# Decoder kernel, one core: order of key powers, residual bases, first table and first values in attention 1, and where the gate's exponential is computed

## The chip, the cores and the metric

The kernel runs on one core of one Trainium2 chip. The metric is the time of one execution in device microseconds. TensorE (PE) multiplies and transposes into PSUM, VectorE (DVE), ScalarE (ACT) and GpSimd (POOL) work element by element, SyncE (SP) issues most transfers. Every engine takes its own instructions in order and waits at semaphores.

## The reference

Six sub-layers, each followed by a layer norm over the last axis, on x of 8 batches x 128 tokens x 128 features, all float32. The change touches the first three.

```python
x = _layernorm(x + _L0_attn_ref(x, ...))       # returns x + attention(LN(x)) @ w_out + b_out
x = _layernorm(x + _L0_xattn_ref(x, ctx, ...)) # q, k layer-normed per head of 8; context of 77 rows
x = _layernorm(x + _L0_ffn_ref(x, ...))        # 8 experts, 2 chosen per batch from the mean token
x = _layernorm(x + _L1_attn_ref(x, ...))       # router: attention for 32 tokens, a scan for 96
x = _layernorm(x + _L1_xattn_ref(x, ctx, ctx, mask, ...))
x = _layernorm(x + _L1_ffn_ref(x, ...))
```

Both attentions have 16 heads of 8 features and a softmax. In the first, the input of the layer norm is 2x + b_out + product. In the second, each key's 8 features are scaled with 1/sqrt(variance + eps) of their head: 77 rows x 8 batches x 16 heads, that is 128 columns of 77 rows. The third takes `gate = softmax(mean(x) @ gate_w.T)`, the two largest of eight, normalised.

## The kernel before, in words

All work of the first attention (`at1`) is a loop over 8 batches, written out by hand on each engine (`attention_tensor`, `attention_vector`, `attention_scalar`, `attention_pool`). In step i, TensorE computes `shifted(i)` (scores less their maxima, L1443 and L1446), `weigh(i-1)` (exponentials by values, L1462), `flips(i)` (projection of batch i-3, L1473, and transposes of the maxima of batch i+1, L1477, and of the normalised output of batch i-2, L1480), `scores(i+2)` (L1422), and transposes outputs (L1508). VectorE in step i makes, in this order: R of batch i-3 (L974, residual base XB plus projection), the maxima of batch i+2 (L952) with the reciprocal and normalisation of batch i-1 (L983, L995) between them, the first remainder (L962), X of batch i-4 (L1004, needs `rstd` from GpSimd), the second remainder (L962), then the statistics of R down to the variance `ve` (L1010 to L1012). `between` holds further work for the end of a step: `key_variances` (L932, L935), `weights2`, `weights5`. ScalarE takes the exponentials (L641), outT (L652) and the flipped maxima (L657).

GpSimd runs one queue: constants and zeroed values, `spread8` (L520), `residual1` (whole XB = 2x + b, L540, L541), `key_squares` (L526, after the last context copy), three key powers of 32 columns (L534, each waits for `k_ss`), then `attention_pool(at1, ...)`: the power for `rstd` of each batch (L504) and behind those of batches 0 and 1 a key power of 16 columns. After it come the query squares (L557), `residual2` (whole XB = X + bp2, L546), `attention_pool(at2)` and the column mask (L562 and the selection behind it).

In the opening, TensorE transposes x and the context, makes q1, k1 and both halves of v1 (L1391), then the scores of batch 0; three context products (`kv.0` to `kv.2`, L1391 again), the scores of batch 1, the first flip; then step 0, in which the last context product stands. ScalarE copies x0T and ctxT (L614), k1 with the head mask (L620), kv.0 to kv.2 (L683, L684), and only then the first flip (L657). VectorE copies q1 (L1036) and v1 (L1039). A ring (`Ring`) hands PSUM banks to fill/copy pairs in the order of `ACT_JOBS` and `DVE_JOBS`; a fill waits until the last copy from its bank is done.

In the gated mixture VectorE ranks the 8 logits (L1094 to L1107) while ScalarE loads the exponential's table, computes `e8`, and loads the Gelu table again (L726 and the loads around it); VectorE makes `c8` (L1115); TensorE spreads it (L1627, L1630). Meanwhile TensorE has done `residual(0)` (L1620) and two of four hidden products of the second half (L1385), the other two come after `residual(1)`.

## Time and profile before

| | us |
|---|---|
| median of 3 runs | 433.56 (433.10 to 434.45) |
| the profiled execution, its own time | 434.33 |
| its span in the profile | 432.5 |

| engine | busy us | share |
|---|---|---|
| PE | 391.3 | 90% |
| DVE | 280.9 | 65% |
| ACT | 235.6 | 54% |
| POOL | 130.5 | 30% |

The profile is of one execution. 1.83 us of its time lie outside the span. A timeline line gives the start from the start of the span, the length of the group, the engine, the line of the kernel, the instruction, what it writes from what, and in brackets how long the engine sat idle before it and what ended that. A group of several instructions (x4) is one line; the engine need not be busy between them. The share of busy time of TensorE holds filler matmuls too (L1371), which the kernel issues to keep the engine's clock up.

### The profile page before, as it was taken

To read this page: it belongs to the slowest core of one execution; us is meant where nothing else is said; L and a number is where in the kernel's file an instruction comes from. 1 tells how busy PE (TensorE), PEld (TensorE's weight loads), DVE (VectorE), ACT (ScalarE), POOL (GpSimd) and SP (SyncE) were. 2 spreads that over 40 slices of the span, in tenths; PEclk is the share of its full clock that TensorE was granted. 3 is DMA by queue.
4 is the path that set the end of the run, shared out by engine and by line. 5 is a ranking of instruction groups with operands and counts; after the bars stand their busy time and mean duration, and the time that the engine had idled before them with its cause. 6 is when DMAs were issued, how large, how long until landed. Compare 5 with 4: busy or idle time off the path is not lost.

```text
span 432.5 us, 10063 instructions
## 1 busy us (share of the span) xinstructions
PE 391.3 (90%) x4041; PEld 262.1 (61%) x4050; DVE 280.9 (65%) x705; ACT 235.6 (54%) x441; POOL 130.5 (30%) x120
## 2 busy tenths in 40 slices
PE   5989798889999999977999999898999899999992
PEld 2556566546675946555676767645777466666662
DVE  6769656754765586897799897732566544444446
ACT  1855444736668267799999993025555442222220
POOL 6936952300113050004889893100011100000001
PEclk9999979999999999999999999989999999999998
DMA  6320000000000000020223220450000000000001
GB/s 176 74 49 2 4 2 2 1 2 3 3 5 0 2 0 2 6 109 23 90 89 102 93 81 2 131 163 2 3 4 4 2 0 0 2 0 1 2 0 48
DMA packets 16881, 13.84 MB, mean 32 GB/s; under 512 B 6548, under 2 KB 14133, under 8 KB 16837
## 3 DMA queue, kind: packets, MB, share of 16 engines
q1 hardware_dynamic: 15538, 12.51, 10.0%
q10 hardware_dynamic: 1299, 0.71, 0.5%
q8 instruction: 32, 0.52, 0.5%
q14 instruction: 12, 0.10, 0.1%
HBM read 12.64 MB, written 0.57 MB: 31 GB/s over the span
## 4 chain that ended last, share of the span: by engine, by line
PE 69%; ACT 11%; DVE 10%; POOL 5%; issue 4%; POOLq 0%; DVEq 0%; ACTq 0%
PE PS L1830 9%; PE PS L1909 6%; PE PS L1913 6%; PE PS L1940 6%; PE PS L1385 5%; PE PS L1443 5%; PE PS L1817 4%; POOL hr L534 4%; ACT att L641 3%; PE PS L1422 3%; PE PS L1371 2%; PE PS L1391 2%; PE PS L1508 2%; PE PS L1462 2%; ACT outT L652 2%
## 5 line engine op out<-in xcount | busy, mean ns | idle before, releaser
L641 ACT ACTIVATE att<-PS 77x512 f32<-77x512 f32 (+1 forms) x96 | 51.7, 591 | 47.2 <-PE PS L1446 47.2
L952 DVE TENSOR_REDUCE mxp<-PS 128x4 f32<-128x308 f32 (+1 forms) x96 | 48.0, 536 | 34.3 <-PE PS L1422 34.3
L878 ACT ACTIVATE kM<-PS 128x512 f32<-128x512 f32 x32 | 19.1, 597 | 55.5 <-PE PS L1909 54.4
L504 POOL TENSOR_TENSOR rstd<-ve,neg_half 128x1 f32<-128x1 f32 x24 | 13.1, 547 | 114.6 <-DVE ve L1012 114.6
L1258 DVE TENSOR_TENSOR_SCAN big<-big,PS 128x768 f32<-128x768 f32 x22 | 38.1, 1743 | 3.4 <-PE PS L1817 3.3
L1324 DVE TENSOR_TENSOR big<-kM,PS 128x512 f32<-128x512 f32 x32 | 21.9, 687 | 27.3 <-PE PS L1913 26.0
L498 POOL TENSOR_TENSOR rstd<-ve,neg_half 128x4 f32<-128x4 f32 x6 | 6.2, 1029 | 102.2 <-DVE ve L908 102.2
L1909 PE MATMUL PS<-xT,V 128*128 128x512 f32 x64 | 33.0, 597 | 1.1 <-DVE xT L1312 0.8
L1913 PE MATMUL PS<-xT,V 128*128 128x512 f32 x64 | 32.7, 592 | 0.0
L1940 PEld LDWEIGHTS PS<-big 128*128 128x128 f32 x256 | 29.7, 192 | 3.3 <-issue 3.3
L1371 PE MATMUL PS<-negsel,identb 128*128 128x512 bf16 x101 | 26.1, 400 | 6.1 <-DVE negsel L1024 4.4
L1940 PE MATMUL PS<-big 128*128 128x128 f32 x256 | 29.7, 275 | 0.0
L1446 PE MATMUL PS<-flipped,negsel 32*77 32x128 bf16 (+1 forms) x384 | 24.8, 219 | 0.0
L831 ACT ACTIVATE att<-big,BT 128x256 f32<-128x256 f32 x58 | 24.6, 497 | 0.0
L534 POOL TENSOR_TENSOR hr<-hvar,half_bh 77x32 f32<-77x32 f32 (+1 forms) x5 | 22.0, 4419 | 7.0 <-DVE hvar L935 7.0
L1345 DVE SCALAR_TENSOR_TENSOR R<-PS,aff,R 128x128 f32<-128x128 f32 x56 | 15.8, 345 | 11.2 <-PE PS L1940 11.2
L1443 PE MATMUL PS<-qT,kM 32*77 32x128 f32 x512 | 20.8, 276 | 1.8 <-ACT att L641 1.1
L1371 PEld LDWEIGHTS PS<-negsel,identb 128*128 128x128 bf16 x109 | 10.4, 102 | 19.1 <-issue 4.9
L1913 PEld LDWEIGHTS PS<-xT,V 128*128 128x128 f32 x64 | 12.2, 190 | 15.3 <-issue 14.8
L657 ACT ACTIVATE flipped<-PS 128x128 f32<-128x128 f32 (+1 forms) x33 | 10.7, 325 | 18.2 <-PE PS L1477 10.0
L1817 PE MATMUL PS<-ident,att 128*128 128x128 f32 x128 | 19.3, 273 | 1.2 <-ACT att L831 1.2
L1258 DVE TENSOR_TENSOR_SCAN untransposed<-untransposed,PS 128x768 f32<-128x768 f32 x10 | 17.5, 1748 | 4.4 <-PE PS L1817 4.1
(368 smaller groups left out, 894.6 us busy)
## 6 DMA issues: line engine op xcount, KB each, us to landing
kM<-Cdram SPq DMA_DIRECT2D x6, 384.0 KB, 3.5
XH<-Cdram SPq DMA_DIRECT2D x5, 384.0 KB, 3.3
xT<-Cdram SPq DMA_DIRECT2D x5, 384.0 KB, 3.4
V<-in_L_ffn_Wg SPq DMA_DIRECT2D x1, 1024.0 KB, 5.4
V<-in_L_ffn_Wu SPq DMA_DIRECT2D x1, 1024.0 KB, 8.0
out_x<-X SPq DMA_DIRECT2D x2, 256.0 KB, 2.3
ctxN<-in_ctx ACTq DMA_DIRECT2D x1, 308.0 KB
X<-in_x ACTq DMA_DIRECT2D x1, 256.0 KB, 4.0
```

The source lines that it names most:

```text
L534: P_.tensor_tensor(out=hr1[0:NC, n], in0=hvar[0:NC, n], in1=half_bh[0:NC, 0:n.stop - n.start], op=ALU.pow)\
L641: A_(PT[0:nk, i % 2, g], bank4(at.bank("exp", i, g), nk), ACT.Exp, scale=at.scale)\
L952: V_.tensor_reduce(mxp[:, b % 3, g, 0:J], PS[:, at.bank("max", b, g), 0:J * nk].rearrange("p (j k) -> p j k", j=J), axis=AX.X, op=ALU.max) ...
L1258: V_.tensor_tensor_scan(hst[m % NHS], dA[m % NDA], dBu[m % NDB], 0.0, ALU.mult, ALU.add)\
L1371: M_(PS[:, bank, :], identb[:], negsel[:].rearrange("p j t -> p (j t)"), start=True, stop=True)
L1443: M_(PS[0:nk, at.bank("exp", b, g), j * T:(j + 1) * T], at.kM[rows(g), j, b, :], qT[rows(g), b, :], start=not at.masked, stop=False)
L1446: ins = M_(PS[0:nk, at.bank("exp", b, g), j * T:(j + 1) * T], negsel[rows(g), j, 0:nk], upper(flipped)[rows(g), (b - 1) % 2, 0:T], start=F ...
L1817: ins = nc.tensor.transpose(dBu[n % NDB][:, 128 * k:128 * (k + 1)], scaled[s % 2][k][:, 128 * h:128 * (h + 1)], ident[:])
L1830: ins = M_(y_piece(h, lo, hi), ident[:], hC[n % NHC][:, lo:hi], start=False, stop=(n // NH == DS - 1 and (h, lo) != (0, 512)))
L1909: M_(PS[:, n % 2, :], Wg6[:, e, i * 128:(i + 1) * 128], half(xT, c), start=True, stop=True)\
L1913: M_(PS[:, 2 + n % 2, :], Wu6[:, e, i * 128:(i + 1) * 128], half(xT, c), start=True, stop=True)\
L1940: ins = M_(PS[:, 4 + (2 * e + c) % 4, b4 * D:(b4 + 1) * D], hidE[e % 2][:, i, b * T:(b + 1) * T], Wd6[:, NI * e + i, :], start=(i == 0), s ...
```

## The change

1. `K_PARTS` is two parts of 32 and four of 16 (before: three of 32, two of 16). GpSimd computes two parts ahead of `attention_pool(at1)` and one behind the `rstd` of each of batches 0 to 3. VectorE makes the key variances at the end of step 0 (before: step 1).
2. `residual1(b)` makes the base of one batch; batch 0 ahead of the key squares, batch b+1 behind the `rstd` of batch b. R of batch r waits for r+1 of them. `residual2(b)` makes the base of the second attention by batch, behind the X of that batch; both run on GpSimd inside `attention_pool(at1)`.
3. ScalarE loads the exponential's table at its start.
4. The second half of the values, v1.1, is multiplied after the first scores and copied on VectorE after the maxima of batch 0; TensorE waits for that copy ahead of the scores of batch 1. The third context product moves behind the scores of batch 1; the first flip follows it.
5. GpSimd computes `e8` as e to the power g (new tile `base8`); ScalarE's two table loads around its own go. The four hidden products of the second half stand together ahead of `residual(0)`.
6. The column mask is made ahead of `attention_pool(at2)`.

```diff
--- before.py
+++ after.py
@@ -45,7 +45,7 @@
 EPS = 1e-5
-K_PARTS = [(0, 32), (32, 64), (64, 96), (96, 112), (112, 128)]
+K_PARTS = [(0, 32), (32, 64)] + [(n, n + 16) for n in range(64, B * H, 16)]
 class Ring:
@@ -161,8 +161,8 @@
                 pe.wait_ge(self.max_ready if before == "max" else self.exp_ready, G * k + slot + 1)
-ACT_FIRST = {"x0T.0": 2, "ctxT.0": 0, "x0T.1": 3, "ctxT.1": 1, "k1.0": 2, "k1.1": 7, "kv.0": 6, "kv.1": 5, "kv.2": 6, "kv.3": 6}
-DVE_FIRST = {"q1.0": 4, "q1.1": 5, "v1.0": 6, "v1.1": 4}
+ACT_FIRST = {"x0T.0": 2, "ctxT.0": 0, "x0T.1": 3, "ctxT.1": 1, "k1.0": 2, "k1.1": 7, "kv.0": 6, "kv.1": 4, "kv.2": 6, "kv.3": 6}
+DVE_FIRST = {"q1.0": 4, "q1.1": 5, "v1.0": 6, "v1.1": 5}
 ACT_JOBS = (list(ACT_FIRST)
             + ["x2T.0"] + [f"hid.{t}.0" for t in range(4)] + ["x2T.1"] + [f"hid.{t}.1" for t in range(4)]
@@ -406,7 +406,7 @@
     dpos = qc
     hid = big[:, 0:4 * B * T].rearrange("p (t n) -> p t n", t=4)
-    pooledT = sb("pooledT", [128, B]); ones_col = sb("ones_col", [128, 1]); e8 = sb("e8", [8, 8]); s8 = sb("s8", [8, 1])
+    pooledT = sb("pooledT", [128, B]); ones_col = sb("ones_col", [128, 1]); e8 = sb("e8", [8, 8]); base8 = sb("base8", [8, 8]); s8 = sb("s8", [8, 1])
     g8 = sb("g8", [8, 8]); m8 = sb("m8", [8, 1]); c8 = sb("c8", [8, 8]); t64 = sb("t64", [8, 8, 8]); e64 = sb("e64", [8, 8, 8])
@@ -466,6 +466,7 @@
         P_.memset(onesb[:], 1.0)
         P_.memset(ones_col[:], 1.0)
+        P_.memset(base8[:], math.e)
         P_.memset(upb3[:], 0.0).then_inc(event("upb_zero"), 1)
         affine(ident[:], ALU.not_equal, [[-1, 128]]).then_inc(const_ready, 1)
@@ -504,10 +505,7 @@
                 P_.tensor_tensor(out=rstd[:, b:b + 1], in0=ve[:, b:b + 1], in1=neg_half[:, 0:1], op=ALU.pow)\
                 if later:
-                    later()
-        def wide(bias):
-            return bias[:].rearrange("p (o n) -> p o n", o=1).to_broadcast([128, B, D])
+                    later(b)
         pool.wait_ge(event("xh1"), 2)
@@ -534,36 +532,43 @@
             P_.tensor_tensor(out=hr1[0:NC, n], in0=hvar[0:NC, n], in1=half_bh[0:NC, 0:n.stop - n.start], op=ALU.pow)\
-        def residual1():
-            loaded(pool, "x0", "x1", "l2")
-            step(P_.tensor_tensor(out=XB[:], in0=X[0][:], in1=X[0][:], op=ALU.add))
-            P_.tensor_tensor(out=XB[:], in0=XB[:], in1=wide(bo1), op=ALU.add).then_inc(at1.xb_ready, 1)
-        def residual2():
-            loaded(pool, "l2")
-            P_.tensor_tensor(out=XB[:], in0=X[1][:], in1=wide(bp2), op=ALU.add).then_inc(at2.xb_ready, 1)
-        residual1()
+        def residual1(b):
+            step(P_.tensor_tensor(out=XB[:, b, :], in0=X[0][:, b, :], in1=X[0][:, b, :], op=ALU.add))
+            P_.tensor_tensor(out=XB[:, b, :], in0=XB[:, b, :], in1=bo1[:], op=ALU.add).then_inc(at1.xb_ready, 1)
+        def residual2(b):
+            pool.wait_ge(at1.x_ready, b + 1)
+            P_.tensor_tensor(out=XB[:, b, :], in0=X[1][:, b, :], in1=bp2[:], op=ALU.add).then_inc(at2.xb_ready, 1)
+        def first_steps(b):
+            if b + 1 < B:
+                residual1(b + 1)
+            if b < 4:
+                key_rstds()
+            if b >= 1:
+                residual2(b - 1)
+        loaded(pool, "x0", "x1", "l2")
+        residual1(0)
         key_squares()
-        for _ in range(3):
+        for _ in range(2):
             key_rstds()
-        steps = iter([key_rstds, key_rstds])
-        attention_pool(at1, lambda: next(steps, lambda: None)())
+        attention_pool(at1, first_steps)
+        residual2(B - 1)
         P_.tensor_tensor(out=sq[:, 0:HB], in0=qc[:, 0:HB], in1=qc[:, 0:HB], op=ALU.mult).then_inc(event("q_sq"), 1)
-        pool.wait_ge(at1.x_ready, B)
-        residual2()
+        step(P_.memset(colmask[:], 0.0))
+        step(affine(colmask[:].rearrange("p j (g i d) -> p j g i d", g=G, i=J), ALU.not_equal,
+                    [[1, J], [0, G], [-1, J], [0, HD]], 0))
         attention_pool(at2)
-        step(P_.memset(colmask[:], 0.0))
-        affine(colmask[:].rearrange("p j (g i d) -> p j g i d", g=G, i=J), ALU.not_equal, [[1, J], [0, G], [-1, J], [0, HD]], 0)\
-            .then_inc(event("colmask"), 1)
-        pool.wait_ge(event("colmask"), 1)
+        pool.wait_ge(dring.copied, dring.index["logits8"] + 1)
+        P_.tensor_tensor(out=e8[:], in0=base8[:], in1=g8[:], op=ALU.pow).then_inc(event("gate3_exp"), 1)
         pool.wait_ge(at2.pv_done, B)
         pool.wait_ge(event("proj_ones"), 1)
@@ -668,6 +673,8 @@
             A_(table_out[:, k:k + 1], eps_col[:], func)
         load(act, "x1", "ctx", "kv2")
+        act.wait_ge(const_ready, 1)
+        table(ACT.Exp)
         loaded(act, "ln1")
         for c in range(2):
@@ -676,7 +683,6 @@
         act.wait_ge(event("small"), 1)
         masked("k1.1", lambda j: kM1[:, j, HB:B, :], bank4, headmask, mb1)
-        table(ACT.Exp)
             kv = PS[0:NC, aring.take(act, f"kv.{p}"), :].rearrange("p (b n) -> p b n", b=2)
@@ -721,9 +727,6 @@
         copy_out("x2T.1", half(xT, 1), bank4)
-        table(ACT.Exp)
-        dring.wait_copied(act, "logits8")
-        A_(e8[:], g8[:], ACT.Exp).then_inc(event("gate3_exp"), 1)
         activated(1)
@@ -969,8 +972,8 @@
                     dve.wait_ge(at.proj_ready, r + 1)
                         dve.wait_ge(at.flipped_copied, i + 2)
-                    if r == 0 and not at.masked:
-                        dve.wait_ge(at.xb_ready, 1)
+                    if not at.masked:
+                        dve.wait_ge(at.xb_ready, r + 1)
                     V_.tensor_tensor(R[:, r, :], at.XB[:, r, :], PS[:, at.bank("flip", i), 2 * T:3 * T], ALU.add)\
                 if ahead:
@@ -1034,12 +1037,13 @@
         centre(Wkv2[:, 0:D], 0).then_inc(event("w2_centred"), 1)
             V_.tensor_scalar(half(qT, c), bank4(take(f"q1.{c}")), bqk1[:, 0:1], None, ALU.add).then_inc(dring.copied, 1)
-        for c in range(2):
-            i = take(f"v1.{c}")
+        def value_copy(c):
             V_.tensor_tensor(V1[:, c * HB:(c + 1) * HB, :, 0:HD],
-                             bank4(i).rearrange("p b (h d) -> p b h d", h=H),
+                             bank4(take(f"v1.{c}")).rearrange("p b (h d) -> p b h d", h=H),
                              bv1[:].rearrange("p (o h d) -> p o h d", o=1, h=H).to_broadcast([128, HB, H, HD]),
                              ALU.add).then_inc(dring.copied, 1)
+        value_copy(0)
@@ -1066,7 +1070,7 @@
         def key_variances():
-        attention_vector(at1, {1: key_variances, 2: weights2, 3: weights5})
+        attention_vector(at1, {-2: lambda: value_copy(1), 0: key_variances, 2: weights2, 3: weights5})
         dve.wait_ge(event("k_rstd"), len(K_PARTS))
@@ -1529,8 +1533,11 @@
             aring.wait_copied(pe, f"x0T.{c}")
             product(aring, f"k1.{c}", Wqkv1[:, D:2 * D], half(xT, c))
-        for c in range(2):
+        def first_values(c):
             row_products(dring, f"v1.{c}", [xT[:, b, :] for b in range(c * HB, (c + 1) * HB)], Wqkv1[:, 2 * D:3 * D])
+        first_values(0)
             for p in ps:
@@ -1541,14 +1548,16 @@
             dring.wait_copied(pe, "q1.0")
         def contexts():
+            first_values(1)
             pe.wait_ge(event("w2_centred"), 1)
             dring.wait_copied(pe, "v1.0")
-            context_products(0, 1, 2)
-            aring.wait_copied(pe, "k1.1", "kv.1")
-            dring.wait_copied(pe, "q1.1")
-        def values_copied():
+            context_products(0, 1)
+            aring.wait_copied(pe, "k1.1")
             dring.wait_copied(pe, "v1.1")
+        def contexts_copied():
+            context_products(2)
+            aring.wait_copied(pe, "kv.1")
             context_products(3)
@@ -1566,7 +1575,7 @@
             transposes("gate3T", [gate3[:]], E0, 128)
         attention_tensor(at1, {B + 1: x1_half, B + 2: mixture_weights}, 0,
-                         [keys_ready, contexts, values_copied, lambda: None, last_context])
+                         [keys_ready, contexts, contexts_copied, lambda: None, last_context])
         transposed_half("x1T", 1, X[1], at1.x_ready, HB, idle=11)
@@ -1619,8 +1628,8 @@
             ups.append(fill(dring, f"up.{c}"))
+        hidden(1, range(4))
         residual(0)
-        hidden(1, (0, 1))
         pe.wait_ge(event("c8_ready"), 1)
@@ -1629,7 +1638,6 @@
         ins.then_inc(dring.full, 1)
         residual(1)
-        hidden(1, (2, 3))
         dring.wait_copied(pe, "cT")
```

## Rows read from the trace of the kernel before

**Rows 1.** The chain of waits, 27 to 53 us: start, length, what.
```profile
36.36 16.22 POOL hr L534 x3
```
**Rows 2.** Timeline in attention 1, VectorE then TensorE: start, length, instructions [idle before <-releaser].
```profile
46.95 0.29 DVE L974 TENSOR_TENSOR R<-XB,PS 128x128 f32<-128x128 f32 x1
...
50.00 0.17 DVE L962 TENSOR_TENSOR mxp<-mxp 128x16 f32<-128x16 f32 x1
...
53.13 0.35 DVE L1004 TENSOR_SCALAR X<-R,mv,rstd 128x128 f32<-128x128 f32 x1 [2.96 <-POOL rstd L504]
...
54.02 0.15 DVE L1012 TENSOR_SCALAR ve<-mv 128x1 f32<-128x1 f32 x1
...
53.62 0.47 PE L1477 MATMUL PS<-ident,mxp 128*128 128x128 f32 x1 [2.52 <-DVE mxp L962]
...
57.30 0.81 PE L1443 MATMUL PS<-qT,big 32*128 32x128 f32 x8
```
**Rows 3.** One stretch: busy us by engine (instructions), granted clock, DMA share, GB/s.
```profile
54.00:58.00 4.00, 4.00 (x26) 1.88 (x28) 1.73 (x5) 1.36 (x3) 4.00 (x3) 0.50 0.00 0
```
**Rows 4.** GpSimd's instructions by shape: busy us, mean ns of one, idle before.
```profile
L504 POOL TENSOR_TENSOR rstd<-ve,neg_half 128x1 f32<-128x1 f32 x24 | 13.1, 547 | 114.6 <-DVE ve L1012 114.6
...
L534 POOL TENSOR_TENSOR hr<-hvar,half_bh 77x16 f32<-77x16 f32 x2 | 5.8, 2906 | 0.0
...
L557 POOL TENSOR_TENSOR sq<-qc 128x512 f32<-128x512 f32 x1 | 1.0, 1039 | 3.6 <-PE PS L1380 3.6
...
L540 POOL TENSOR_TENSOR XB<-X 128x1024 f32<-128x1024 f32 x1 | 1.9, 1882 | 0.0
...
L583 POOL TENSOR_SCALAR kM<-ident,Dp 128x128 f32<-128x128 f32 x2 | 1.2, 609 | 0.0
```
**Rows 5.** Timeline, batches 0 and late: VectorE, GpSimd, TensorE.
```profile
45.60 0.15 DVE L1012 TENSOR_SCALAR ve<-mv 128x1 f32<-128x1 f32 x1
...
65.97 0.29 DVE L974 TENSOR_TENSOR R<-XB,PS 128x128 f32<-128x128 f32 x1 [1.96 <-ACT flipped L657]
...
67.72 0.15 DVE L1012 TENSOR_SCALAR ve<-mv 128x1 f32<-128x1 f32 x1
...
70.20 0.29 DVE L974 TENSOR_TENSOR R<-XB,PS 128x128 f32<-128x128 f32 x1
...
71.80 0.28 DVE L974 TENSOR_TENSOR R<-XB,PS 128x128 f32<-128x128 f32 x1
...
71.96 0.55 POOL L504 TENSOR_TENSOR rstd<-ve,neg_half 128x1 f32<-128x1 f32 x1 [1.07 <-DVE ve L1012]
...
72.36 2.32 PE L1371 MATMUL PS<-negsel,identb 128*128 128x512 bf16 x10 [0.89 <-DVE R L974]
```
**Rows 6.** Timeline of the opening: ScalarE, TensorE, VectorE.
```profile
9.23 1.28 ACT L614 ACT_TABLE_LOAD   x1 [9.23 <-PE PS L1380]
...
21.14 0.37 ACT L684 ACTIVATE V<-PS 77x256 f32<-77x256 f32 x1
...
22.20 0.28 ACT L657 ACTIVATE flipped<-PS 128x128 f32<-128x128 f32 x1 [0.68 <-PE PS L1477]
...
16.84 1.14 PE L1422 MATMUL PS<-big,qT 32*128 32x512 f32 x8
...
17.91 2.92 PE L1391 MATMUL PS<-Wkv,ctxT 128*77 128x256 f32 x12
...
16.05 0.69 DVE L1039 TENSOR_TENSOR big<-PS,bv 128x512 f32<-128x512 f32 x1 [1.00 <-PE PS L1391]
...
20.52 1.18 DVE L962 TENSOR_TENSOR mxp<-mxp 128x16 f32<-128x16 f32 x2
```
**Rows 7.** Timeline of TensorE in the gated mixture.
```profile
138.74 0.63 PE L1627 MATMUL PS<-ident,c 8*64 8x8 f32 x16 [0.45 <-DVE c L1115]
```
**Rows 8.** Timeline before attention 2: VectorE, then ScalarE.
```profile
80.62 1.00 DVE L935 TENSOR_SCALAR hvar<-hss 128x128 f32<-128x128 f32 x1
...
80.95 0.39 ACT L710 ACTIVATE hr<-hss,eps_col 128x128 f32<-128x128 f32 x1
```

## The prediction

> **What bounds the kernel now.** I read the page's chain first (TensorE owns 69% of it), then looked for the places inside the changed stretches where the chain leaves TensorE. The largest is in attention 1: the chain rows show one GpSimd item of 16.22 us, three key powers of 32 columns in a row, starting at 36.36 [rows 1]. The reciprocal root of batch 0 (L504) stands behind them in GpSimd's queue. So VectorE, done with the remainder at 50.17, waits 2.96 us at its X instruction until 53.13, and TensorE, whose transpose needs VectorE's next instruction, waits 2.52 us until 53.62 [rows 2]. After that wait the granted clock is 0.50, the 1.2 GHz level, in the whole of 54 to 58 us [rows 3]. The shifted scores of batch 6 then begin only at 57.30 [rows 2]. What this costs is about 4 us: 3 us until those scores, as the sum below shows, and what the low clock adds to them. From about 69 us the steps are short and VectorE is never far ahead: R of batch 6 starts at 70.20, R of batch 7 at 71.80, 1.60 us apart [rows 5]. TensorE's busy filler ahead of the next stage is released by that last R (72.36) [rows 5].
>
> **Key powers and residual bases (the main part).** The change moves two things on GpSimd's queue. The powers start about 5 us sooner, since the key variances move from VectorE's step 1 to step 0; two of 32 columns (16.22/3 = 5.41 us each) then end near 42, ahead of the first variance of attention 1, which is there at 45.75 [rows 1, 5]. So the 2.96 us stall at X goes. But four parts of 16 columns (2.91 us each) are left for batches 0 to 3, and the residual base of batch b+1 (two adds of 128x128, the second behind a wait for the first) now runs behind the power of batch b. VectorE's R of batch b+1 waits for it. In the kernel before, that base was whole from the start and R followed the variance at once (the row at 71.80 starts beside the end of the previous variance; the power starts at 71.96, 0.1 us behind it) [rows 5].
>
> The price of a 128x128 add on GpSimd has no row. Nearest are 1.88 us for 128x1024 and 1.04 us for 128x512 [rows 4]: the line through both gives 0.20 + 0.00165 per column, 0.41 us. The lower bound is an eighth of the 1024-wide one, 0.24; the upper is the 128x128 multiply with a scalar, 0.61 [rows 4]. I take 0.41. From a variance to R of the next batch it is then 0.09 (semaphore) + 0.51 (the power, 0.55 less overlap with what follows) + 0.41 + 0.08 + 0.41 + 0.05 = 1.55 us. (The Trainium skill's GPSIMD Engine Reference, section 3.1, gives 2.6 cycles per element for a two-input add; 128 columns would be an estimated 0.28 us without dispatch, which lies near the lower bound. The two rows here agree with a cheaper column but a fixed part; by 0.28 the sum below would be about 2 us smaller.)
>
> Now the chain. VectorE takes 4.26 us from R to the variance in a step with maxima (46.95 to 50.17, then 53.13 to 54.17) [rows 2], about 1.75 to 1.9 in steps 6 to 8 (65.97 to 67.87) and about 1.2 in the last two, which have R, X and the statistics only [rows 5].
> - R1 = 45.75 + 1.55 = 47.3 (before 46.95); variance 1 at 51.57; R2 at 53.1; the shifted scores of batch 6 follow a maximum about 1.16 us behind R, at 54.3 in place of 57.30: 3 us won, and the low clock's loss behind it (some 1.3 us in that step) too.
> - Variance 2 at 57.4, R3 at 58.95, variance 3 at 60.7. But GpSimd has been in a 2.91 us key part since 58.9, and then does the base of attention 2 for one batch (0.41): free at 62.2. Power and base: R4 at 63.7 (before 65.97).
> - Variance 4 at 65.6; GpSimd, again behind a key part and a base, is free at 66.95; R5 at 68.45.
> - Variance 5 at 70.2, R6 = 71.75 (before 70.20); variance 6 at 72.95, R7 = 74.5 (before 71.80).
> So the about 4.3 us won by step 6 are spent: 1.5 us each in two steps on the key parts, then 1.1 to 1.5 us in each of the last ones on the loop of power, two adds and R. Net +2.7 us at R7, with what hangs on it. With adds of 0.24 the same chain gives R7 at 71.8 (no change), with 0.61 it gives 77.7 (+5.9).
>
> **The clock behind it.** In this chain TensorE has nothing between about 65.7 (projection of batch 6) and 69.4 (the normalised output of batch 7 comes behind R5), and again from about 72 until R7: two waits of over 3 us, where 2.52 us was followed by clock 0.50 before [rows 2, 3]. The filler of 10 to 11 matmuls, 2.32 us from 72.36 at the high clock [rows 5], and the two products behind it would start at the low level. Nothing to all of a recovery like the one from 53.6 to 60 (half of 6.4 us): 0 to +3.2; I take +1.8.
>
> **The opening.** The first activation waits behind a table load of 1.28 us at 9.23; loading it while the engine is idle brings the first copy 1.3 us and the query product 1.0 us forward [rows 6]. The second half of the values leaves TensorE's queue ahead of the first scores, so these can start near 15.4 in place of 16.84. But the second scores now wait for that second value copy, and it stands behind the first maxima and both remainders. Maxima end at 15.4 + 3.65 = 19.05; the remainders took 1.18 us for two, where one alone takes 0.17 [rows 2, 6]; the copy takes 0.65 of its 0.69 [rows 6]: second scores at 20.1 to 20.9, where they began at 20.76. A third context product (2.92/3 = 0.97 us) [rows 6] and its two ACT copies (0.37 each, 0.65 together as they overlap) now stand between these scores and ACT's copy of the first flip, which started at 22.20: it now starts at 23.0 to 23.8. Everything behind it moves, so +0.6 to +1.3; if the remainders and ACT run unhindered and the scores' gain survives, it could be -0.85. I take +0.8. A rule bears on this: the 1.18 us fell while GpSimd ran its first wide add, and the Trainium skill's SBUF — State Buffer, "SBUF: two separate sides", says that GpSimd and a VectorE operation with two SBUF inputs hold a shared port pair one at a time, for a whole instruction. The trace agrees as far as it goes (0.8 us more than twice the single remainder). The wide adds leave this place, but in the changed order the spread multiply, ahead of them on GpSimd, would run at that moment.
>
> **Small items.** (a) The whole residual base of attention 2 no longer runs beside the query statistics: hvar took 1.00 us at 80.62; but the reciprocal behind it needs ACT's root, which ends at 81.34, so of 0.78 only 0.27 comes back [rows 8]. (b) The column mask leaves the end of attention 2, where it shares GpSimd and the port with the last X: nothing to 0.2, taken as 0.1. (c) Gate: two table loads go, GpSimd computes e to the g for 8 columns: 0.39 + 8 x 0.156 = 1.6 us on the line of the 1-column and 16-column powers [rows 4], as late as ACT's result was. TensorE now does four hidden products first and waits uncovered for the copy of x2T that its identity product used to cover; it saves the 0.45 us wait ahead of 138.74 [rows 7] and then runs without a gap as before. Bounds -0.5 and +0.6, taken as nothing: it trades one short wait for another. Together about -0.35.
>
> **Sum.** +2.7 + 0.8 + 1.8 - 0.35 = +4.95 us on the profiled execution of 434.33 us, 439.3; that execution stands 0.77 above the median of 433.56, so 438.5 us.
>
> **Rivals.**
> 1. The clock holds through the two waits (they are short of what turns it down). Then +2.7 + 0.8 - 0.35 = +3.15: 436.7. For it: only one such wait is in the trace. Against: 2.5 us sufficed there.
> 2. Faster: the small adds cost near their share, 0.24 us, so GpSimd's loop of 1.2 us costs just what the removed stall gives back, the two waits shrink and the clock holds, and the opening keeps its gain: 0 - 0.85 - 0.35 = -1.2, 432.4. It decides at an add of about 0.27. Against it: the 0.20 us fixed part between the 512- and 1024-wide rows.
> 3. About the same: adds near 0.3 (R7 +0.9), opening +0.2, clock held, less 0.35: +0.75, 434.3.
> 4. That the powers don't start sooner (squares wait for the last context copy, then VectorE's sums find its queue blocked): the stall at X returns in part and the loop costs as well: about 441.
>
> **How the numbers follow.** Forecast 0.50, its own range 435.5 to 441.0; rival 1 0.18; rival 2 0.18; rival 3 0.10; rival 4 0.04. A measurement of this kernel can tell about 0.3%, 1.3 us. Slower by more: 0.50 + 0.18 + 0.04, less 0.02 for forecasts that fall short = 0.70; within: 0.12; faster: 0.18, and the low bound 432.4 takes in the price of rival 2. The high bound, 441.2, takes in an add of 0.5 with the low clock.
>
> **What would show it.** VectorE's X of batch 0 without a wait, the shifted scores of batches 5 and 6 about 6 us apart, clock 1.0 from 53 to 62: stall gone. R of batches 4 to 7 each ended by GpSimd's XB add, and the last two R 2.7 us apart: the loop. GpSimd's adds near 0.41. TensorE's filler ahead of the second x1T at clock 0.5. The flip's ACT copy later than 22.2. Wrong if R waits for ACT's flipped copies or for nothing, or if the adds are near 0.25.

## The result, and the profile after

The changed kernel is slower by 1.4%: its median is 439.53 us (438.56 to 439.97, 4 runs), against 433.33 us (431.92 to 434.45, 4 runs) for the kernel before. The ratio is 1.0142, with a 95% interval of 1.0107 to 1.0177. The forecast was 438.5, between 432.4 and 441.2, with "slower" the likeliest sign. The profiled execution took 439.23 us, the one of before 434.33, so the difference to explain between the two profiles is 4.9 us (spans 437.2 and 432.5, 4.7 us). That is less than the 6.2 us between the medians; the account of the sum below says where the rest lies.

The page of the changed kernel, its span and the busy time of each engine:

```profile
span 437.2 us, 10084 instructions
...
PE 391.7 (90%) x4041; PEld 264.0 (60%) x4050; DVE 279.1 (64%) x705; ACT 233.4 (53%) x437; POOL 136.7 (31%) x144
```

These shares say nothing about the cause. The way to find it is to take the same instruction in both traces, at the end of each changed stretch, and to subtract. The step from one such anchor to the next is what the stretch between them cost:

| anchor | before, us | after, us | difference | step |
|---|---|---|---|---|
| first flipped copy of ScalarE starts | 22.20 | 23.42 | +1.22 | |
| variance of batch 0 in attention 1 is there | 45.75 | 46.78 | +1.03 | +1.03 |
| last R of attention 1 starts | 71.80 | 75.70 | +3.90 | +2.87 |
| TensorE's filler behind it starts | 72.36 | 76.28 | +3.92 | +0.02 |
| transposes of the query half (q2T) start | 85.16 | 88.76 | +3.60 | -0.32 |
| last X of attention 2 ends | 134.01 | 137.45 | +3.44 | -0.16 |
| first bias products of the gated mixture start | 142.08 | 145.96 | +3.88 | +0.44 |
| value copies ahead of the scan start | 193.75 | 197.61 | +3.86 | -0.02 |
| first scan starts | 197.90 | 202.65 | +4.75 | +0.89 |

More than half of the loss is in attention 1. Its late batches in the changed kernel, VectorE first and then GpSimd (timeline: start, length, instruction, in brackets the idle time before it and what ended it):

```profile
51.69 0.34 DVE L1007 TENSOR_SCALAR X<-R,mv,rstd 128x128 f32<-128x128 f32 x1
...
54.39 0.29 DVE L977 TENSOR_TENSOR R<-XB,PS 128x128 f32<-128x128 f32 x1 [1.67 <-POOL XB L538]
...
64.91 0.29 DVE L977 TENSOR_TENSOR R<-XB,PS 128x128 f32<-128x128 f32 x1 [3.07 <-POOL XB L538]
...
69.61 0.29 DVE L977 TENSOR_TENSOR R<-XB,PS 128x128 f32<-128x128 f32 x1 [3.06 <-POOL XB L538]
...
72.92 0.29 DVE L977 TENSOR_TENSOR R<-XB,PS 128x128 f32<-128x128 f32 x1 [1.67 <-POOL XB L538]
```
```profile
64.74 2.91 POOL L532 TENSOR_TENSOR hr<-hvar,half_bh 77x16 f32<-77x16 f32 x1
67.61 0.45 POOL L543 TENSOR_TENSOR XB<-X,bp 128x128 f32<-128x128 f32 x1
68.03 0.56 POOL L505 TENSOR_TENSOR rstd<-ve,neg_half 128x1 f32<-128x1 f32 x1
68.55 0.40 POOL L537 TENSOR_TENSOR XB<-X 128x128 f32<-128x128 f32 x1
69.03 0.45 POOL L538 TENSOR_TENSOR XB<-XB,bo 128x128 f32<-128x128 f32 x1
...
71.33 0.56 POOL L505 TENSOR_TENSOR rstd<-ve,neg_half 128x1 f32<-128x1 f32 x1 [1.44 <-DVE ve L1015]
```

In the kernel before the corresponding R instructions of the last batches waited for nothing [rows 5]. Here each R of batches 1 to 7 waits for GpSimd. In the short loop it waits 1.67 us: the power (0.56), the first add (0.40), the second add (0.45) and the gaps between them. With a key part in GpSimd's queue it waits 3.06 us: the variance of batch 4 is there at 66.55, but the power starts at 68.03, behind a key part that ends at 67.65 and behind a base of attention 2. TensorE's side of the same stretch, and the granted clock there (stretch and its length, busy us of TensorE, its weight loads, VectorE, ScalarE and GpSimd with their instructions, clock, DMA share, GB/s):

```profile
70.45 0.47 PE L1484 MATMUL PS<-ident,oN 128*128 128x128 f32 x1 [3.45 <-DVE oN L998]
...
76.28 2.32 PE L1375 MATMUL PS<-negsel,identb 128*128 128x512 bf16 x10 [2.17 <-DVE R L977]
```
```profile
54.00:58.00 4.00, 3.05 (x84) 2.51 (x84) 3.58 (x11) 1.17 (x3) 3.55 (x3) 1.00 0.00 0
...
66.00:70.00 4.00, 0.97 (x7) 0.57 (x5) 0.87 (x5) 0.28 (x1) 3.81 (x6) 0.70 0.00 0
70.00:72.00 2.00, 1.55 (x8) 1.56 (x9) 1.15 (x6) 0.47 (x2) 0.67 (x2) 0.50 0.00 0
72.00:74.00 2.00, 2.00 (x10) 1.67 (x9) 1.01 (x5) 1.06 (x3) 1.13 (x3) 0.50 0.04 8
74.00:76.00 2.00, 0.11 (x1) 0.01 (x1) 0.37 (x3) 0.61 (x2) 1.77 (x4) 0.90 0.01 4
76.00:78.00 2.00, 1.73 (x8) 0.89 (x10) 1.27 (x6) 0.00 (x0) 0.98 (x3) 1.00 0.00 0
```

The low clock of [rows 3] is gone from 54 to 58 us. A low stretch now lies at about 67.6 to 74.4 us: the mean of 0.70 from 66 to 70 us is 2.4 us at half clock, and the 0.90 from 74 to 76 us is 0.4 us. TensorE's wait of 3.45 us runs from 67.00 to 70.45, so the clock fell 0.6 us into it, not behind it. The low stretch is over when the filler starts, and the filler takes the 2.32 us that it took before [rows 5].

### The profile page after: what moved, and what is told of

It is laid out like the page before. It is cut to its first block, busy times and chain, and to the rows that moved or that the text cites. A ratio compares the mean times of both kernels' runs of the same rounds, so it can differ in the third digit from the quotient of the medians.

```text
span 437.2 us, 10084 instructions
## 1 busy us (share of the span) xinstructions
PE 391.7 (90%) x4041; PEld 264.0 (60%) x4050; DVE 279.1 (64%) x705; ACT 233.4 (53%) x437; POOL 136.7 (31%) x144
## 4 chain that ended last, share of the span: by engine, by line
PE 69%; DVE 11%; ACT 10%; POOL 4%; issue 4%; POOLq 0%; DVEq 0%; ACTq 0%
PE PS L1838 9%; PE PS L1917 6%; PE PS L1921 6%; PE PS L1948 6%; PE PS L1389 5%; PE PS L1447 5%; PE PS L1825 4%; PE PS L1426 3%; ACT att L646 3%; PE PS L1466 2%; PE PS L1375 2%; DVE mxp L955 2%; PE PS L1384 2%; PE PS L1395 2%; PE PS L1512 2%
## 5 line engine op out<-in xcount | busy, mean ns | idle before, releaser
L532 POOL TENSOR_TENSOR hr<-hvar,half_bh 77x16 f32<-77x16 f32 (+1 forms) x6 | 22.5, 3750 | 1.8 <-DVE hvar L938 1.8
```

## Experiments

Each kernel is the one before, or the changed one, with one part of the change put in or taken out. The table gives what the readings below rest on: the anchors in the profiled execution of each kernel, in us. One execution each is behind these rows, and where the low clock falls in it is in them; the times under each heading are of all its executions.

| kernel | flipped copy | variance 0 | last R | variance 0 to last R | q2T | bias product | scan | span |
|---|---|---|---|---|---|---|---|---|
| before | 22.20 | 45.75 | 71.80 | 26.05 | 85.16 | 142.08 | 197.90 | 432.5 |
| changed | 23.42 | 46.78 | 75.70 | 28.92 | 88.76 | 145.96 | 202.65 | 437.2 |
| e1_whole_base | 25.74 | 51.01 | 72.66 | 21.65 | 86.06 | 143.26 | 199.08 | 433.6 |
| e2_two_ahead | 23.42 | 46.79 | 70.53 | 23.74 | 85.21 | 142.41 | 197.94 | 431.2 |
| e3_keys_alone | 22.30 | 45.85 | 66.67 | 20.82 | 80.03 | 136.97 | 193.12 | 427.6 |
| e4_opening_alone | 26.43 | 49.80 | 75.79 | 25.99 | 89.16 | 146.09 | 201.94 | 436.6 |
| f1_keys_table_early | 21.11 | 44.66 | 65.47 | 20.81 | 78.84 | 135.76 | 192.44 | 427.0 |
| f2_opening_early | 22.70 | 46.15 | 72.16 | 26.01 | 85.54 | 142.46 | 198.28 | 433.0 |
| g1_good_parts | 20.93 | 44.49 | 65.30 | 20.81 | 79.13 | 135.53 | 191.53 | 426.3 |
| g2_bases_alone | 22.20 | 45.75 | 80.07 | 34.32 | 94.82 | 151.74 | 208.44 | 443.1 |

### The key powers alone

The kernel before, with the key parts and their earlier start, and the residual base whole as it was:

```diff
-K_PARTS = [(0, 32), (32, 64), (64, 96), (96, 112), (112, 128)]
+K_PARTS = [(0, 32), (32, 64)] + [(n, n + 16) for n in range(64, B * H, 16)]
...
-        for _ in range(3):
+        for _ in range(2):
             key_rstds()
-        steps = iter([key_rstds, key_rstds])
+        steps = iter([key_rstds] * 4)
...
-        attention_vector(at1, {1: key_variances, 2: weights2, 3: weights5})
+        attention_vector(at1, {0: key_variances, 2: weights2, 3: weights5})
```

> The kernel before with the key powers alone: two parts of 32 and four of 16, key variances one step sooner, all else as before. Theory: the 2.96 us wait at X of batch 0 and the low clock behind it go, nothing takes their place: 4 us faster than before, 429 to 430. Rival: the parts of 16 between the batches' powers make X of batches 2 to 4 late and give half of it back: 431 to 432.

Measured: 429.43 us (426.94 to 429.87, 10 runs), ratio 0.9904 [0.9874, 0.9935] to the kernel before on the same chip (432.97 us, 31 runs). The stretch from variance 0 to the last R takes 20.82 us where it took 26.05. VectorE's R of batches 2 to 4 now wait for ScalarE's flipped copies, which is attention's own work:

```profile
51.94 0.29 DVE L974 TENSOR_TENSOR R<-XB,PS 128x128 f32<-128x128 f32 x1 [0.72 <-ACT flipped L657]
57.18 0.29 DVE L974 TENSOR_TENSOR R<-XB,PS 128x128 f32<-128x128 f32 x1 [0.71 <-ACT flipped L657]
60.84 0.29 DVE L974 TENSOR_TENSOR R<-XB,PS 128x128 f32<-128x128 f32 x1 [1.96 <-ACT flipped L657]
```

So this part does what it says and is worth 5.2 us in its stretch, about 4 in the total. The two differ in part by the clock. The gate kernels below have the same stall at X as the kernel before (TensorE waits 2.53 and 2.54 us), but the clock was low behind it for 3.4 us in place of 6.8, and the stretch took 24.7 and 24.8 us in place of 26.05. Against those two profiles the keys are worth 3.9 us. What the changed kernel lost, it lost elsewhere.

### The residual bases alone

The kernel before with the base made batch by batch, keys and opening untouched:

```diff
-        residual1()
+        def first_steps(b):
+            if b + 1 < B:
+                residual1(b + 1)
+            if b < 2:
+                key_rstds()
+            if b >= 1:
+                residual2(b - 1)
+        residual1(0)
...
-        attention_pool(at1, lambda: next(steps, lambda: None)())
+        attention_pool(at1, first_steps)
...
-                    if r == 0 and not at.masked:
-                        dve.wait_ge(at.xb_ready, 1)
+                    if not at.masked:
+                        dve.wait_ge(at.xb_ready, r + 1)
```

> The kernel before with the residual bases by batch alone (both attentions), one batch ahead behind the powers as in the changed kernel; key powers as before. Theory (loop): now R of batch 1 as well as X of batch 0 stands behind the three 32-column powers, and every later R 1.73 us behind the variance before it: R of batches 1 to 7 at 54.0, 59.9, 65.9, 69.3, 72.7, 76.1 and 78.9 (71.8 before), about 7 us slower than before, 439 to 441. Rival: the bases are hidden as long as GpSimd has gaps of over 1 us between its powers, as it has from batch 2 on, and only batch 1 is late: 434 to 435.

Measured: 445.20 us (442.79 to 445.45, 4 runs), ratio 1.0276 [1.0222, 1.0331] to 432.90 us on the same chip. The R instructions show what stood in the way (VectorE, timeline):

```profile
54.12 0.29 DVE L981 TENSOR_TENSOR R<-XB,PS 128x128 f32<-128x128 f32 x1 [7.20 <-POOL XB L540]
61.18 0.29 DVE L981 TENSOR_TENSOR R<-XB,PS 128x128 f32<-128x128 f32 x1 [2.91 <-ACT flipped L664]
67.38 0.29 DVE L981 TENSOR_TENSOR R<-XB,PS 128x128 f32<-128x128 f32 x1 [1.67 <-POOL XB L540]
70.69 0.29 DVE L981 TENSOR_TENSOR R<-XB,PS 128x128 f32<-128x128 f32 x1 [1.67 <-POOL XB L540]
```

The stall of [rows 2] was 2.96 us because R of batch 1 could go ahead of the power of batch 0. With the base behind that power the whole wait falls on R, 7.20 us, and from there each batch pays the 1.67 us. R of batch 1 came where it was expected, the later ones 1.2 to 1.5 us behind. The excess arises in the one step from 54 to 61 us, where R waits for ScalarE and the granted clock is 0.50 (52 to 60 us). The time misses the 439 to 441 us expected by over 4 us: 1.2 us are in the last R, 1.6 in the filler below and 0.9 where the scan starts (5.04 us behind the value copies, for 4.15 before); the small rest isn't accounted for. At the end the loop's latency keeps TensorE idle again, and here the filler did start at the low level (TensorE's timeline, then the stretch):

```profile
80.73 3.92 PE L1378 MATMUL PS<-negsel,identb 128*128 128x512 bf16 x10 [3.89 <-DVE R L981]
```
```profile
80.00:84.00 4.00, 3.27 (x8) 1.33 (x10) 2.68 (x7) 0.00 (x0) 2.71 (x4) 0.57 0.00 0
```

It takes 3.92 us for ten matmuls in place of 2.32, 1.6 us more, close to the 1.8 us that the prediction had put on this place in the changed kernel. In attention 1 the two parts nearly add up: keys alone -5.23 us, bases alone +8.27, opening alone -0.06 from variance 0 to the last R, sum +2.98; measured together +2.87. The agreement is of sizes and not of mechanism: the base loses 7.20 us at one R here, behind three powers that the changed kernel has moved, and there it loses in two waits of over 3 us behind key parts.

### The whole base in the changed kernel

```diff
-            step(P_.tensor_tensor(out=XB[:, b, :], in0=X[0][:, b, :], in1=X[0][:, b, :], op=ALU.add))
-            P_.tensor_tensor(out=XB[:, b, :], in0=XB[:, b, :], in1=bo1[:], op=ALU.add).then_inc(at1.xb_ready, 1)
+            step(P_.tensor_tensor(out=XB[:], in0=X[0][:], in1=X[0][:], op=ALU.add))
+            P_.tensor_tensor(out=XB[:], in0=XB[:], in1=bo1[:].rearrange("p (o n) -> p o n", o=1).to_broadcast([128, B, D]), op=ALU.add).then_inc(at1.xb_ready, B)
...
-            if b + 1 < B:
-                residual1(b + 1)
```

> The changed kernel with one edit taken back: the base 2x + b of attention 1 is made whole, ahead of the key squares, as in the kernel before. Theory (loop): R of batch b+1 waited for two adds behind the power of batch b; without it no R waits for GpSimd, the removed stall stays removed, and the last R, at 75.7 us in the changed kernel, comes at 68.8 (71.8 of before, plus 1.0 from the opening, less 4.0): about 6.5 us faster than the changed kernel, 431 to 433. Rival (key parts): the late batches were held by the 16-column powers that stand between the batches' powers, and the adds only rode along; then R of batches 4 and 5 stay late and the time falls by no more than 1 to 2 us, to 437 to 438.

Measured: 435.54 us (434.72 to 436.79, 10 runs), ratio 1.0067 [1.0039, 1.0094]. That misses the 431 to 433 expected, although the stretch in question behaves as expected: 21.65 us from variance 0 to the last R, 7.3 less than in the changed kernel. The variance of batch 0 itself comes 4.2 us later (51.01 for 46.78). The opening shows why (VectorE's two maxima remainders, then ScalarE's flipped copy):

```profile
19.10 2.58 DVE L963 TENSOR_TENSOR mxp<-mxp 128x16 f32<-128x16 f32 x2
...
25.74 0.27 ACT L660 ACTIVATE flipped<-PS 128x128 f32<-128x128 f32 x1
```

The two remainders take 2.58 us in place of 1.10, beside GpSimd's wide add (19.55 to 21.43), and everything of the new order waits for them: the second value copy, then the second scores. TensorE waits 3.00 us until 22.38 and then runs at the low level from 24 to 28 us (0.50) and into the next stretch (0.78 from 28 to 34). I had not seen that the base's wide form and the new opening touch. The next kernel isolates it.

### The opening alone

The kernel before with the first table at the start, the second half of the values behind the first scores, and its copy behind the first maxima; base whole, keys as before:

```diff
+        act.wait_ge(const_ready, 1)
+        table(ACT.Exp)
...
-        attention_vector(at1, {1: key_variances, 2: weights2, 3: weights5})
+        attention_vector(at1, {-2: lambda: value_copy(1), 1: key_variances, 2: weights2, 3: weights5})
...
         def contexts():
+            first_values(1)
...
-            context_products(0, 1, 2)
+            context_products(0, 1)
...
+        def contexts_copied():
+            context_products(2)
```

> The kernel before with the opening alone: first table at the start, second half of the values behind the first maxima, third context product behind the second scores. Theory: ScalarE's copy of the first flip, 22.20 us before, comes at 23.4, the shifted scores of batch 0 follow it, and all behind them is 1.0 us later: 434.3 to 434.8. Rival: the later stall at X (GpSimd's three powers) swallows or passes on only a part: 433.5 to 434.

Measured: 435.75 us (432.70 to 438.43, 10 runs), ratio 1.0065 [1.0029, 1.0102]. The time misses the 434.3 to 434.8 expected. Variance 0 is 4.05 us later than in the kernel before, not 1.0:

```profile
18.55 1.03 POOL L520 TENSOR_TENSOR spread<-spread,ident 8x512 f32<-8x512 f32 x1
...
18.88 2.80 DVE L963 TENSOR_TENSOR mxp<-mxp 128x16 f32<-128x16 f32 x2
...
19.55 1.88 POOL L540 TENSOR_TENSOR XB<-X 128x1024 f32<-128x1024 f32 x1
...
21.60 0.68 DVE L1039 TENSOR_TENSOR big<-PS,bv 128x512 f32<-128x512 f32 x1
...
23.86 1.99 PE L1393 MATMUL PS<-Wkv,ctxT 128*77 128x256 f32 x4
```

The two remainders, 0.17 us each when nothing is in the way [rows 2], sit through the spread multiply and through the wide add. In the changed kernel the same rows are these:

```profile
18.88 1.10 DVE L965 TENSOR_TENSOR mxp<-mxp 128x16 f32<-128x16 f32 x2
...
19.55 0.39 POOL L537 TENSOR_TENSOR XB<-X 128x128 f32<-128x128 f32 x1
...
19.90 0.68 DVE L1041 TENSOR_TENSOR big<-PS,bv 128x512 f32<-128x512 f32 x1
...
21.75 1.09 PE L1395 MATMUL PS<-Wkv,ctxT 128*77 128x256 f32 x4
```

The flipped copy is 3.0 us later here than in the changed kernel (26.43 for 23.42). Of these, 1.7 us are the remainders' longer wait, which is on the value copy and on the second scores behind it. The other 1.3 us are the clock: TensorE waited 3.22 us for that copy, the clock was low from 23.0 to 26.4 us, and the third context product took 1.99 us for 1.09. So the small base shields the new opening: the residual base by batch costs its 1.67 us for each batch later, and saves these 3.0 us. The two parts can't be priced apart and added. The profiled execution is the slowest of the ten, 2.7 us above their median, so the 3.0 us need not be typical of what the collision costs.

### The opening without the collision

The same as the last kernel, with the spread multiply and the whole base moved ahead of GpSimd's zeroing of the value rows, where they end before the first maxima:

```diff
         pool.wait_ge(event("xh1"), 2)
+        P_.tensor_tensor(out=spread8[:].rearrange("p (e c) -> p e c", e=E0), ..., op=ALU.mult)
+        residual1()
         value_ones(V1)
...
-        residual1()
         key_squares()
```

> The kernel before with the whole opening of the change (table, values behind the first maxima, third context product behind the second scores) and GpSimd's spread multiply and whole base moved ahead as in the run above. Theory: with the base where it was, the opening cost 4 us because the remainders waited 2.8 us for GpSimd's wide add; without that the remainders take 0.38 us, but the chain remainders - value copy - second scores - third context product - its copies - first flip is still longer than before: flip's copy at 22.9 to 23.1 (22.2 before), so 0.7 us slower than before: 433.3 to 434.5. Rival (the port was all of it): flip's copy at 21.5 or sooner and 1 us faster than before.

Measured: 431.78 us (430.15 to 434.80, 10 runs), ratio 0.9995 [0.9959, 1.0031] to 432.08 us (19 runs) on its chip. The median misses the 433.3 to 434.5 expected; the profiled execution, at 434.80, is the slowest of the ten. The remainders take 0.38 us for both, with GpSimd zeroing beside them, so a GpSimd instruction that only writes didn't hold them. The flipped copy starts at 22.70, 3.7 us sooner than in the kernel with the collision, and still 0.5 later than before:

```profile
18.87 0.38 DVE L963 TENSOR_TENSOR mxp<-mxp 128x16 f32<-128x16 f32 x2
...
22.15 0.38 ACT L684 ACTIVATE qc<-PS 77x256 f32<-77x256 f32 x1 [2.31 <-PE PS L1393]
22.70 0.27 ACT L657 ACTIVATE flipped<-PS 128x128 f32<-128x128 f32 x1
```

What stands ahead of the flipped copy is the copy of the third context product, as the prediction said. So the new place of the values is a loss of 0.5 us at this anchor even with the collision gone, and of 1.6 us against the next kernel. The whole time can't show the 0.5: its ratio has 1 in its interval.

(The Trainium skill's SBUF — State Buffer, "SBUF: two separate sides", has both halves of this: a VectorE operation with two SBUF inputs and a GpSimd operation that reads SBUF hold the port pair one at a time, each for its whole instruction. The trace agrees: 2.80 us beside the multiply and the wide add, 0.38 beside the zeroing.)

### Keys and table, without moving the values

The key powers, the early table and the early base, values where they were:

```diff
+        act.wait_ge(const_ready, 1)
+        table(ACT.Exp)
...
+        residual1()
         value_ones(V1)
```

> The kernel before with the key powers of the change, the first table at the start, and GpSimd's spread multiply and whole residual base moved ahead of the zeroing of the values (from 18.6 - 23.9 us to about 9.5 - 15), so that no two-input operation of GpSimd runs when VectorE makes the first remainders. Values stay where they were. Theory (port): the two first remainders take 0.38 us in place of 1.18, the first flip's copy comes at 21.2 in place of 22.2, and the whole is 1.0 us faster than the key powers alone: 428 to 429. Rival: the adds, now beside the context centring and the query copies, hold VectorE up there and nothing is won over the key powers alone: 429 to 430.

Measured: 428.44 us (425.94 to 429.46, 10 runs), ratio 0.9906 [0.9875, 0.9936]. The flipped copy starts at 21.11, 1.6 us ahead of the last kernel's, which is the price of the values' move alone. Variance 0 is there at 44.66, 1.2 us sooner than with the keys alone. The scan starts only 0.7 us sooner: the granted clock is 0.50 from 179 to 183 us here, and 1.00 in the same products with the keys alone. The ratios of the two kernels are equal (0.9906 and 0.9904), so by them the early table and base give nothing. They mix executions of different mean clock, though. At a mean granted clock of 0.983 this kernel took 428.8 to 429.5 us (5 executions) and the keys alone 429.6 to 429.9 (3); at 0.987 and 0.988 it took 427.9 and 428.0, the keys alone 429.4 to 429.5 (3). That points to a gain of about 1 us, the size of the anchor's 1.2.

### Two bases ahead

The changed kernel with the base of batch b+2, not b+1, behind the power of batch b:

```diff
-            if b + 1 < B:
-                residual1(b + 1)
+            if b + 2 < B:
+                residual1(b + 2)
...
         residual1(0)
+        residual1(1)
         key_squares()
```

> The changed kernel with the same adds by batch, but two batches ahead: the bases of batches 0 and 1 are made ahead of the key squares, and behind the power of batch b stands that of batch b+2. GpSimd's work is the same to the instruction. Theory (loop): what costs is the latency variance - power - add - add - R, so a slack of one batch takes most of it away; only GpSimd's occupation in batches 3 and 4 is left, 1 to 2 us: 432 to 434. Rival (occupation): GpSimd's sum of work is the price, and the time stays within 1 us of the changed kernel, 438.5 to 439.5.

Measured: 434.15 us (432.45 to 435.79, 10 runs), ratio 1.0024 [0.9995, 1.0053]; that is about 5 us less than the changed kernel, with the same work on every engine. The stretch from variance 0 to the last R takes 23.74 us in place of 28.92. So 5.2 us of the changed kernel are pure order, R waiting for adds that could have been made a step sooner. The 2.9 us between 23.74 and the keys-alone kernel's 20.82 are left for the adds' own time in GpSimd's queue, among the key parts: the X instruction at 67.75 waits 2.54 us for its power, where the longest such wait with the keys alone is 0.66. And once more the filler pays, behind a long wait:

```profile
70.88 3.71 PE L1376 MATMUL PS<-negsel,identb 128*128 128x512 bf16 x11 [3.60 <-DVE R L978]
```

Eleven matmuls take 2.55 us at the high level (keys alone), 3.71 here. The clock fell only at 72.1 us, 1.2 us after the filler had started (mean 0.76 from 70 to 74 us).

### The gate

The kernel before with the gate's power on GpSimd, the mask ahead of attention 2 and four hidden products ahead of the identity product:

```diff
+        pool.wait_ge(dring.copied, dring.index["logits8"] + 1)
+        P_.tensor_tensor(out=e8[:], in0=base8[:], in1=g8[:], op=ALU.pow).then_inc(event("gate3_exp"), 1)
...
+        hidden(1, range(4))
         residual(0)
-        hidden(1, (0, 1))
```

> The kernel before with the gate of the change: e to the power g on GpSimd, ScalarE's two table loads gone, column mask ahead of attention 2, and the four hidden products together ahead of the identity product. Theory: GpSimd's power is as late as ScalarE's exponential was, and TensorE waits 0.75 us for the copy of x2T with nothing to do: from the end of the last X of attention 2 to the bias products of the mixture 8.5 us where it was 8.07. Rival: the removed table loads shorten it to 7.6 or less.

And the same with the identity product first:

```diff
-        hidden(1, range(4))
         residual(0)
+        hidden(1, range(4))
```

> As the run above, but the identity product of the first half stays first and the four hidden products follow it, so that it covers the wait for the copy of x2T. Theory: both short waits are gone, from the end of the last X to the bias products 7.6 us where it was 8.07 and 8.5 in the changed order. Rival: GpSimd's result comes too late for it, or the products wait for ScalarE's copies: 8.0 or more.

Measured, one run each: 432.08 and 431.31 us, too near to the 432.08 of the kernel before for the times to tell. The stretch from the last X of attention 2 to the first bias products does tell: 8.53 us and 7.73, where it took 8.07 before and 8.51 in the changed kernel. TensorE, in the order of the change and then in the other:

```profile
135.57 3.67 PE L1383 MATMUL PS<-xT,down3T 128*128 128x512 f32 x8 [0.76 <-ACT xT L615]
```
```profile
134.80 1.12 PE L1618 MATMUL PS<-X,ident 128*128 128x512 f32 x2
...
135.76 3.60 PE L1383 MATMUL PS<-xT,down3T 128*128 128x512 f32 x8
```

The hidden products need the copy of x2T and wait 0.76 us for it, uncovered. The identity product needs none, and fills that wait. With the identity product first this part gains 0.34 us on the kernel before; the change's order costs 0.80 of it.

### The good parts together

Keys, table and base early, GpSimd's gate power with the identity product first; values where they were:

```diff
         residual(0)
-        hidden(1, (0, 1))
+        hidden(1, range(4))
```

(on top of the keys-and-table kernel and the gate's power)

> The parts that helped, put together on the kernel before: key powers in two parts of 32 and four of 16 and one step sooner, first table at the start, spread multiply and whole base ahead of the zeroing, column mask ahead of attention 2, e to the power g on GpSimd with the identity product ahead of the four hidden products. Values and bases as before. Theory: 4.0 us of the keys + 1.1 us of the opening + 0.5 us of mask and gate, less up to 1 us that the clock takes where the scan starts: 1.0 to 1.3% faster than before, 427 to 428.5. Rival: the clock takes back what the opening and the gate give, so that the time is that of the key powers alone, 0.95% faster.

Measured: 428.49 us (427.93 to 429.21, 6 runs), ratio 0.9906 [0.9873, 0.9940] to 432.90 us. It beats the kernel before by about 4 us and the changed one by 10 to 11, and has the smallest span of all profiles, 426.3. The ratio is that of the rival named (0.95% faster), and not the 1.0 to 1.3% of the theory. Whether it also beats the keys alone stays open by the ratios: their intervals lie on each other, and the 1.4 us that its variance 0 is sooner are of the size by which one kernel's executions differ (the keys-alone kernel's ten times lie between 426.94 and 429.87). At equal mean clock it is faster: 428.9 to 429.2 against 429.6 to 429.9 us at 0.983, 427.9 to 428.1 against 429.4 to 429.5 at 0.987 and 0.988, three executions of each. Against the keys-and-table kernel it shows no gain in this comparison (428.8 to 429.5 and 427.9 to 428.0).

## Why the prediction was right, and where not

**The stall at X: right.** X of batch 0 runs at 51.69 without a wait; the shifted scores of batches 5 and 6 start at 49.71 and 55.53, 5.8 us apart; the clock is 1.00 where [rows 3] had 0.50. With the keys alone this is 5.2 us.

**The loop: right, in kind and in size.** The forecast was +2.7 us at the last R from the loop and key parts, and +2.87 came. The adds took 0.40 (one operand read twice) and 0.45 to 0.46 (with the bias), where 0.41 was taken between 0.24 and 0.61. From the variance to R the loop took 1.67 us to 1.8, not 1.55, and from R to the next variance VectorE took 4.14 us in the long steps, not 4.26; these two small misses cancel (5.82 us from R to R, 5.81 forecast). The two key-part collisions are the two waits of over 3 us, in the batches that the prediction named. The shape of the chain differed little: R came at 48.57, 54.39, 60.20, 64.91, 69.61, 72.92 and 75.70, each 1.2 to 1.3 us behind the forecast, of which 1.0 is the opening. Rival 2 (adds near 0.24) fell with the measured add. Rival 4 fell with the start of the key powers, 32.19 us in place of 36.36 [rows 1].

**The opening: right in size, half seen in its cause.** +0.8 was forecast, +1.03 came. (The prediction's range for the flipped copy, 23.0 to 23.8, is +0.8 to +1.6 over 22.20, and not the +0.6 to +1.3 that it gives; the copy came at +1.22.) The third context copy ahead of the flipped copy is there: 22.88 and 23.42. That the remainders would wait for the spread multiply was said too (1.10 us for both). What the prediction didn't say is that this moderate loss stands only because the wide adds had gone. With them it was 4.05 us in the profile, low clock included.

**The clock: wrong in its place.** The step that failed is the +1.8 us at the filler. It took two waits of over 3 us as given, though by its own times the second was only 2.5 us (72 to 74.5). The first came out at 3.45 us, and the clock fell in it. The second came out at 2.17 us, because TensorE's side jobs, themselves at the low level, ran on to 74.11. The clock had risen again by the filler. The low stretch from 67.6 to 74.4 us cost nothing, as R of batches 5 to 7 waited for GpSimd and not for TensorE. The term at this place was 0. Rival 1 ("the clock holds", 436.7) was right about this price and wrong about the reason, since the clock did fall in the first wait. The mechanism itself is real: it cost 1.6 us with the bases alone, behind 3.89 us, and 1.2 with two bases ahead, behind 3.60.

**What took its place: +0.89 at the scan, not forecast.** VectorE reaches the value copies with no further loss (197.61), and then waits 2.03 us for ScalarE (L845) ahead of its copy into the scan, where it waited 1.13. TensorE's products from 187.0 to 193.9 us ran at the low level in the changed kernel. VectorE's copy and the stretch, before and then after:

```profile
196.84 0.96 DVE L1262 COPY big<-PS 128x768 f32<-128x768 f32 x1 [1.13 <-ACT att L842]
186.00:196.00 10.00, 7.38 (x67) 5.95 (x57) 8.92 (x16) 9.77 (x17) 0.00 (x0) 0.86 0.14 57
...
201.66 0.96 DVE L1266 COPY big<-PS 128x768 f32<-128x768 f32 x1 [2.03 <-ACT att L845]
186.00:196.00 10.00, 10.00 (x99) 7.69 (x99) 9.14 (x13) 8.52 (x12) 0.00 (x0) 0.66 0.36 120
```

Before, the same stretch of time had 0.86, and its low clock came later, at 193.2 to 196.6 us, where it cost less. More than one pattern occurs in kernels that don't differ there: the distance from the value copies to the scan is 4.15 us before, 5.04 in the changed kernel and 5.03 with keys and table, 4.48 with the keys alone, and 3.9 in three others. So 0.9 us of the changed kernel's loss comes with where the low clock falls, and for how long. That the change brought this about isn't shown; nothing that it edits runs there.

**Small items.** hvar now takes 0.23 us in place of 1.00 [rows 8]; the reciprocal behind it then waits 0.59 us for ScalarE's root, and -0.32 us was left where -0.27 was forecast. The mask away from the end of attention 2 gave -0.16 for -0.1. GpSimd's power of eight columns took 1.68 us for 1.6. The gate was taken as nothing within -0.5 and +0.6, and cost +0.44: the wait for the copy of x2T was named and then set against the gain, when it was the larger of the two.

**The sum.** +2.7, +0.8, +1.8, -0.35 made +4.95. Measured, on the same anchors: +2.9, +1.0, 0, then -0.3 and -0.2 (small items), +0.4 (gate), +0.9 (clock, elsewhere), which is +4.7, the difference of the spans (the profiled times differ by 4.9). The total fits to 0.1 us on the profiled execution, but about a third of it is right by chance: a clock term in the wrong place was made up by one in another and by the gate.

The medians are 6.2 us apart, so the forecast of 438.5 us fell 1.0 short. The mean granted clock of each execution points to where that lies. The kernel before, 61 times on record beside the experiments, took 429.7 to 430.0 us at a mean of 0.991 or 0.992 and 434.1 to 434.5 at 0.979 or 0.980, and its profiled execution is one of the latter. Three of the changed kernel's four executions stand at 0.975 or 0.976 (439.2 to 440.0 us), where only two of those 61 do (436.4 and 436.6). The fourth stands at 0.984 and took 438.56, the kernel before 432.9 to 433.5. At equal mean clock the change thus costs 3 to 6 us. That it lowers the mean clock as well rests on four executions and isn't shown further.

## What to carry to other kernels

A helper engine that is a third busy can still set the end: what counts is how many of its small instructions stand between a result and the next step that needs it, and here one step of slack (bases two batches ahead) gave about 5 us back without a single instruction less. When a reorder moves an instruction with two SBUF inputs, look at which wide read of GpSimd it lands beside, and when one part shrinks such a read, expect the parts not to add up. Cost a fill job by what it covers: the identity product ahead of the hidden products was worth 0.8 us in its stretch. And before a difference of 1 or 2 us between two profiled executions is put down to an edit, compare their mean granted clock with that of the other executions.

## What of the hardware had not been expected

- Two VectorE instructions of 16 columns, 0.38 us together when free, took 2.80 us beside a multiply of 8x512 and an add of 128x1024 on GpSimd, and 0.38 beside GpSimd's zeroing. Each waited for the end of a whole instruction.
- GpSimd's power was priced by its columns, on 128, 77 and 8 partitions alike: 0.56 us for one column on 128, 1.68 for 8 on 8, 2.91 for 16 and 5.41 for 32 on 77. All four lie within 0.05 us of one line, 0.39 us and 0.157 for each column.
- The low level came with TensorE's waits of 2.52, 3.45, 3.60, 3.89 and 7.53 us, but not at one point of them. It began 2.1 us into the first, 0.6 us into the second, 1.2 us after the end of the third, 3.7 us into the fourth and 2.1 us into the last (in the kernel before, the changed one, with two bases ahead, and twice with the bases alone). In the wait of 2.17 us, right behind a low stretch, the clock rose. A low stretch that started earlier here ended in time.
- The low clock at about 177 to 201 us lies in other places and for other lengths from one kernel to the next, without an edit there, and moves the scan by 0.9 us. That is two thirds of the 1.3 us that the prediction took as the least time difference that can be told here, and more than several of the edits are worth. Behind the same stall at X, too, the clock was low for 6.8 us in one execution (53.2 to 60.1) and for 3.4 us in another (53.9 to 57.3).
